# The slot stage of a decoder layer: alpha in one tile, the output product on 64 rows, the division on ScalarE, gelu ahead of the exponential

## The chip, the core and the metric

The kernel runs on one core of a Trainium2 chip. The metric is the device time of one execution in microseconds. The times are medians of repeated executions; a profile is one further execution, with its own time.

## What is computed

A decoder layer on 64 sequences of 128 tokens with 256 features: `x` plus local and latent attention, plus cross attention, plus a slot layer. The change touches the slot layer only, whose input is the normalised `x`:

```python
S = slot_init * slot_scale                      # 64 slots x 256
h = gelu(concat(x, mean(S)) @ w1.T + b1)        # 128 hidden
route_logits = (h @ w2.T + b2) / (abs(tau) + 0.1)
topk_vals, topk_idx = top_k(route_logits, 8)
topk_w = softmax(topk_vals)
alpha = sum(topk_w[..., None] * one_hot(topk_idx, 64), axis=-2)   # tokens x slots
slot_input = einsum('bts,btd->bsd', alpha, x)
gi = slot_input / (alpha.sum(axis=1) + 1e-08)
r, z = sigmoid(xr + hr), sigmoid(xz + hz)       # from gi @ w_ih and S @ w_hh
n = tanh(xn + r * hn)
S_new = (1 - z) * n + z * S
slot_values = S_new @ wv.T + bv
out = einsum('bts,bsd->btd', alpha, slot_values) @ wo.T + bo
```

The layer's result is `x + out`.

## The kernel before

The program has three stages that follow each other on one core: the first attention, the cross attention (its engines end their work some 1479 us after the span's start) and the slot stage, `slots` (L1830 to L2320). `x` stays in SBUF as `x_sb`, [128 tokens, 64 sequences, 256]. The activation and weight tiles are f32.

`slots` first has a block that makes constants: the initial slots, their share in the gates (`rz_const`, `half_hn`, `n_const`), the product `w_vo` of the value and output weights and the value bias through the output weights, `b_vo`. Both halves of the 128 partitions hold the 64 slots, one half for each of two sequences.

Then comes the loop. One step handles pairs of sequences: 32 pairs, and the step for pair `at` also does later parts of the work for the pairs one to four steps back (`at.back(k)`). The functions `step` on each engine set the order by hand; each engine runs its own list in program order, and semaphores join them. `pairs` (L79) unrolls the first eight steps, runs a hardware loop with four steps in its body (`BY = 4`), and unrolls the rest, with `LAST` more steps in which only the older pairs have work.

The life of a pair: VectorE takes the statistics of `x` and scales it to `xn` (L2160), TensorE transposes it (L2021), ScalarE copies it out (`f_xn_t`, L2090), TensorE makes the hidden product (L2029) and ScalarE the gelu (`h_t`, L2101). One step later TensorE makes the logits (L2012); VectorE scales them (L2181), finds the eight largest of each half (`max`, L2187), negates the largest (`neg_top`, L2192) and marks the chosen (L2194); ScalarE takes the exponential (`expd`, L2119); VectorE masks (`chosen`, L2201), sums, inverts, and writes `alpha` (L2211). Two steps back, TensorE makes the slot inputs (L2004), VectorE divides them (`gi`, L2171), TensorE transposes `alpha` (L2049) and `gi` (L2055), ScalarE copies both (`alpha_t`, L2106; `gi_t`, L2112), TensorE makes the gate products (L2063), and VectorE adds the constants (`rz`, L2217). Three steps back, ScalarE takes the tanh (`rz_t`, L2126), GpSimd makes `r_hn` and `r_hn_c` (L2294, L2297), VectorE `n_in` (L2229), ScalarE its tanh `n_out` (L2131), GpSimd `h_n` (L2302), VectorE `z_hn` and `slot_new` (L2233, L2237). Four steps back, TensorE transposes the new slots, multiplies with `w_vo` (L2042), VectorE adds `b_vo` (`slot_val`, L2176), TensorE makes the output (L2072), VectorE adds `x_bias` and writes `y` (L2223), and SyncE stores it (L1991).

`alpha` of one pair is a [128, 2, 128] tile, in which the half that belongs to the other sequence is zero; so its transpose has two blocks of 128 columns, and the output product runs over 128 rows. `x_bias` is `x` plus the output bias, made by GpSimd (L2306). The order of ScalarE's list is this:

```python
for back, what in ((3, gates), (0, copy_xn), (4, copy_slots), (2, copy_alpha),
                   (2, copy_inputs), (3, candidate), (1, exp), (0, gelu)):
```

`gates` is `rz_t` and `candidate` is `n_out`. Between functions whose tables differ the compiler puts an `ACT_TABLE_LOAD`, under the line of the activation that needs it.

Of the kernel before, what the change touches and what calls it, by code (L numbers as in the profile page):

```python
# [7 lines left out]
ALU = mybir.AluOpType  # L8
# [83 lines left out]
def decoder(nc, a, out):  # L92
    with ExitStack() as ctx:
# [12 lines left out]
        with ExitStack() as kept:  # L106
# [6 lines left out]
            with ExitStack() as scope:  # L113
                slots(nc, scope, sem, a, out, bank, x_sb, ident, slot_weights)
# [1715 lines left out]
def slots(nc, scope, sem, a, out, bank, x_sb, ident, w):  # L1830
# [20 lines left out]
    b_vo = sb("b_vo", [128, D])  # L1851
# [38 lines left out]
    x_bias = sb("f_x_bias", [128, 2, D])  # L1890
# [4 lines left out]
    with nc.Block() as block:  # L1895
        @block.vector
        def _(dve):
# [3 lines left out]
            nc.vector.memset(alpha_all[:], 0.0).then_inc(prep_v, 1)  # L1901
# [5 lines left out]
            nc.vector.scalar_tensor_tensor(tau_abs[:], w.tau[:], -1.0, w.tau[:], ALU.mult, ALU.max).then_inc(prep_v, 1)  # L1907
            dve.wait_ge(prep_v, 6)
            nc.vector.tensor_scalar(tau_abs[:], tau_abs[:], 0.1, None, ALU.add).then_inc(prep_v, 1)
            dve.wait_ge(prep_v, 7)  # L1910
            nc.vector.reciprocal(inv_tau[:], tau_abs[:]).then_inc(prep_v, 1)
            dve.wait_ge(prep_v, 8)
# [17 lines left out]
            nc.vector.tensor_copy(b_vo[:], bank[6][:, 0:D]).then_inc(prep_v, 1)  # L1930
            dve.wait_ge(prep_v, 19)

        @block.tensor
        def _(pe):
            pe.wait_ge(prep_v, 4)
# [7 lines left out]
            pe.wait_ge(prep_v, 11)  # L1943
# [15 lines left out]
    tr_bank, hid_bank, logit_bank, in_bank, gate_bank, new_bank, out_bank = (  # L1959
        bank[0], bank[1], bank[2], bank[3], bank[4:6], bank[6], bank[7])  # L1960
# [18 lines left out]
    LAST = 4  # L1979
# [3 lines left out]
    with nc.Block() as block:  # L1983

        @block.sync
        def _(sp):
            def step(at):
                give = at.back(4)
# [9 lines left out]
        def _(pe):  # L1998
            def slot_inputs(at):
                pe.wait_ge(alpha_ready, at.count(2, 2))  # L2000
                wait(pe, giT_ready, at.count(1, 0))
                for tt in range(2):
                    half = slice(SLOTS * tt, SLOTS * tt + SLOTS)
                    mm = pe.matmul(in_bank[half, 0:XW], alpha[at.par][:, tt, half], xn[at.off % BY][:, tt, :],  # L2004
# [81 lines left out]
        def _(act):  # L2086
# [16 lines left out]
            def copy_alpha(at):  # L2103
                act.wait_ge(alphaT_filled, at.count(1, 1))
                wait(act, out_filled, at.count(1, 1 - BY))
                nc.scalar.activation(alpha_t[at.off % BY][:].rearrange("p t n -> p (t n)"), out_bank[:, 0:256],  # L2106
                                     ACT.Copy).then_inc(alphaT_ready, 1)

# [33 lines left out]
        def _(dve):  # L2142
# [21 lines left out]
            def mean_inputs(at):  # L2164
                dve.wait_ge(in_filled, at.count(1, 1))
                nc.vector.tensor_scalar(w_sum[:], in_bank[:, D:XW], 1e-8, None, ALU.add).then_inc(in_step, 1)
                dve.wait_ge(in_step, at.count(3, 1))
                nc.vector.reciprocal(w_inv[:], w_sum[:]).then_inc(in_step, 1)
                dve.wait_ge(in_step, at.count(3, 2))
# [222 lines left out]
```

## Time and profile before

| what | value |
|---|---|
| median of 3 runs | 1788.61 us (1787.81 to 1790.47) |
| the profiled execution's own time | 1789.42 us |
| its span, first to last instruction | 1787.0 us |
| mean granted TensorE clock | 0.972 |
| busy: PE, DVE, ACT, POOL | 1612.1, 1367.5, 967.2, 946.1 us |

The profile names the engines PE (TensorE, with PEld for its weight loads), DVE (VectorE), ACT (ScalarE), POOL (GpSimd) and SP (SyncE). Busy times are sums over the whole span; a stage has to be read from its own stretch. In a timeline a row gives the start, the duration, the engine and line, the operation and its tiles, and in brackets how long the engine had been idle before and what released it. `x4` behind a row says that four records were merged. An f32 matmul has two records.

### The profile page before, as it was taken

What the parts mean: (1) busy time and instruction counts of PE and PEld (TensorE: products, weight loads), DVE (VectorE), ACT (ScalarE), POOL (GpSimd) and SP (SyncE); (2) the same over time, 40 slices, a digit from 0 to 9 for tenths busy, and PEclk for the clock granted to TensorE, in tenths of its full rate; (3) what the DMA queues carried; (4) which work ended last, traced back from release to release, by engine and by line L of the source; (5) the groups of instructions that cost most, each with busy time, mean ns of one, the idle gap of its engine ahead of it and who ended that gap; (6) DMA issues with size and microseconds to landing.
All of it is one profiled execution on the core that took longest, in us unless ns stands there. A gap on an engine that the chain in (4) does not pass through costs nothing. (4 is left out here: it accounts for less than half of the span.)

```text
span 1787.0 us, 52814 instructions
## 1 busy us (share of the span) xinstructions
PE 1612.1 (90%) x18272; PEld 1162.9 (65%) x18334; DVE 1367.5 (77%) x3280; ACT 967.2 (54%) x2049; POOL 946.1 (53%) x1205
## 2 busy tenths in 40 slices
PE   2799999999999999999699999999999976999997
PEld 1566666666666666666477777777777754666664
DVE  4688898989898989898356666666666644898996
ACT  1355555554555555555256565656565633777774
POOL 2345454545555555554336666666666662445544
PEclk9899999999999999999799999999999976999998
DMA  5554455545554455444210000000000000001001
GB/s 102 81 85 87 84 84 84 88 82 83 84 90 82 80 85 91 82 73 80 72 45 14 18 12 18 12 18 12 18 12 18 7 2 1 25 30 35 29 29 41
DMA packets 124323, 92.64 MB, mean 52 GB/s; under 512 B 34849, under 2 KB 122850, under 8 KB 124258
## 3 DMA queue, kind: packets, MB, share of 16 engines
q1 hardware_dynamic: 124258, 91.80, 28.1%
q8 instruction: 38, 0.62, 0.2%
q14 instruction: 27, 0.22, 0.1%
HBM read 23.06 MB, written 8.39 MB: 18 GB/s over the span
## 5 line engine op out<-in xcount | busy, mean ns | idle before, releaser
L1205 POOL TENSOR_SCALAR_AFFINE_SELECT probs_t<-probs_t 128x512 f32<-128x512 f32 x256 | 186.5, 743 | 220.7 <-ACT probs_t L894 220.6
L1682 DVE TENSOR_REDUCE c_neg_max<-score_banks 128x16 f32<-128x2048 f32 x64 | 146.5, 2290 | 100.4 <-PE score_banks L1459 100.3
L1610 ACT ACTIVATE c_probs_t<-score_banks 128x512 f32<-128x512 f32 x256 | 132.2, 603 | 66.0 <-PE score_banks L1485 66.0
L1791 POOL TENSOR_SCALAR_AFFINE_SELECT c_probs_t<-c_probs_t 128x512 f32<-128x512 f32 x256 | 155.4, 643 | 11.8 <-ACT c_probs_t L1610 11.7
L564 PE MATMUL score_banks<-xn_t,w_qk_a 128*128 128x256 f32 x512 | 133.7, 395 | 0.7 <-ACT xn_t L803 0.7
L1482 PE MATMUL score_banks<-c_q_f,c_k_z 32*128 32x128 f32 x2048 | 106.4, 307 | 22.0 <-ACT c_max_t L1603 15.4
L1482 PEld LDWEIGHTS score_banks<-c_q_f,c_k_z 32*128 32x128 f32 x2048 | 92.1, 188 | 45.3 <-ACT c_probs_t L1610 20.1
L713 PE MATMUL bank<-probs_t,v_heads 128*32 128x128 f32 x2048 | 109.2, 285 | 2.7 <-POOL probs_t L1205 0.8
L1042 DVE TENSOR_REDUCE neg_max<-score_banks 128x4 f32<-128x512 f32 x128 | 87.6, 684 | 21.3 <-PE score_banks L625 21.2
L894 ACT ACTIVATE probs_t<-bank 128x512 f32<-128x512 f32 x128 | 76.1, 595 | 41.4 <-PE bank L700 41.3
L564 PEld LDWEIGHTS score_banks<-xn_t,w_qk_a 128*128 128x128 f32 x512 | 91.6, 194 | 10.0 <-ACT xn_t L803 1.1
L1802 POOL TENSOR_TENSOR c_scaled<-c_normed,gamma 128x512 f32<-128x512 f32 x32 | 40.7, 1271 | 97.2 <-DVE c_normed L1665 97.2
L894 ACT ACTIVATE probs_t<-score_banks 128x512 f32<-128x512 f32 x128 | 76.1, 594 | 26.1 <-PE score_banks L700 25.9
L1042 DVE TENSOR_REDUCE neg_max<-bank 128x4 f32<-128x512 f32 x128 | 87.7, 685 | 2.6 <-PE bank L625 1.0
L1696 DVE TENSOR_TENSOR c_v_raw<-bank,b_v_b 128x512 f32<-128x512 f32 x32 | 22.1, 691 | 87.8 <-PE bank L1421 77.9
L2294 POOL TENSOR_TENSOR r_hn<-rz_t,half_hn 128x256 f32<-128x256 f32 x32 | 23.4, 731 | 124.0 <-ACT rz_t L2126 124.0
L2063 PE MATMUL bank<-w_ih,gi_t 128*128 128x512 f32 (+1 forms) x256 | 88.4, 488 | 0.4 <-DVE n_in L2229 0.2
L599 PE MATMUL score_banks<-w_v_a,xn_t 128*128 128x336 f32 x256 | 87.4, 464 | 0.3 <-ACT lat_raw L848 0.3
L1616 ACT ACTIVATE c_av_t<-bank 128x512 f32<-128x512 f32 x64 | 40.0, 625 | 77.7 <-PE bank L1499 77.7
L1572 ACT ACTIVATE c_k_z<-bank,b_k_half,row_half 128x256 f32<-128x256 f32 x128 | 61.9, 564 | 33.1 <-PE bank L1403 33.1
L1016 DVE TENSOR_TENSOR qk_rest<-qk_f,qk_part 128x512 f32<-128x512 f32 x64 | 74.9, 1170 | 6.1 <-ACT qk_f L829 6.1
L1499 PE MATMUL bank<-c_probs_t,c_v_heads 128*32 128x128 f32 x2048 | 74.4, 281 | 2.5 <-POOL c_probs_t L1791 1.8
(266 smaller groups left out, 4692.9 us busy)
## 6 DMA issues: line engine op xcount, KB each, us to landing
q_stack<-qk_part SPq DMA_DIRECT2D x192, 128.0 KB, 3.5
k_stack<-qk_part SPq DMA_DIRECT2D x192, 128.0 KB, 4.6
c_ctx_in<-in_ctx SPq DMA_DIRECT2D x32, 256.0 KB, 2.7
out<-y SPq DMA_DIRECT2D x32, 256.0 KB, 2.1
x_sb<-in_x SPq DMA_DIRECT2D x30, 256.0 KB, 2.7
rq_stack<-lat_part SPq DMA_DIRECT2D x192, 32.0 KB, 2.3
rk_stack<-lat_part SPq DMA_DIRECT2D x192, 16.0 KB, 1.9
w_ih<-in_ffn_w_ih SPq DMA_DIRECT2D x1, 768.0 KB, 5.8
```

The costliest lines, as they stand in the source:

```text
L564: mm = pe.matmul(dst, w(c), src[:, c, :], start=(c == 0), stop=(c == C - 1))
L599: mm = pe.matmul(v_bank[tt][:, 0:n], src[:, c, S * tt:S * tt + S], w_v[:, c, :], start=(c == 0), stop=(c == C - 1))
L713: mm = pe.matmul(av_bank[HW * j:HW * j + HW, 128 * (g % 4):128 * (g % 4) + 128], v_heads[at.par][:, tt, h0 + j, :], probs_t[g % 4][:, j, : ...
L894: nc.scalar.activation(probs_t[g % 4][:].rearrange("p j t -> p (j t)"), score_bank[g % 2][:], ACT.Exp, scale=SCALE).then_inc(exp_done, 1)
L1016: nc.vector.tensor_tensor(rest, src, part[0], ALU.subtract).then_inc(part_step, 1)
L1042: nc.vector.tensor_reduce(neg_max[:, tt, h0:h0 + 4], score_bank[g % 2][:].rearrange("p (j k) -> p j k", k=128), AX.X, ALU.max, negate=True ...
L1205: nc.gpsimd.affine_select(out=pt[:], in_=pt[:], pattern=[[0, 4], [1, 128]], compare_op=ALU.is_ge, fill=0.0, base=-1 if local else 0, chann ...
L1482: pe.matmul(slot(i, j), k_z[at.par][j // 2][group(i), j % 2, toks], q_f[at.par][group(i), j % 2, toks], start=True, stop=False, skip_group ...
L1610: nc.scalar.activation(probs_t[tt][:, 4 * g:4 * g + 4, :].rearrange("p j q -> p (j q)"), score_banks[:, g, :], ACT.Exp, scale=SCALE).then_ ...
L1682: nc.vector.tensor_reduce(neg_max[:, tt, :], all_scores, AX.X, ALU.max, negate=True).then_inc(max_done, 1)
L1791: nc.gpsimd.affine_select(out=heads, in_=heads, pattern=[[0, 4], [1, 128]], compare_op=ALU.is_ge, fill=0.0, base=0, channel_multiplier=-1) ...
L2063: mm = pe.matmul(gate_bank[b][:, 0:hi - lo], gi_t[:, c, :], w.w_ih[:, c, lo:hi], start=(c == 0), stop=(c == C - 1))
```

## The change

In the change the other half of `alpha` is no longer kept: `alpha` is [128, 2, 64], its two halves side by side are one [128, 128] tile, and one transpose gives both, the first sequence's slots on rows 0 to 63 and the second's on rows 64 to 127. The transpose goes into the bank of the slot inputs, behind those of `gi`. The output product of each sequence uses its 64 rows and a bank of its own (`out_bank` is banks 2 and 3; the logits share a bank with the hidden product). The output bias is added to the slot values (`b_all`), and `y` adds `x_sb` itself; GpSimd's `bias_x` goes, and GpSimd negates the largest logit. The division by `w_sum` moves from VectorE to ScalarE (`scale_inputs`). All lists are in a new order, and the output is made five steps back.

```diff
-    b_vo = sb("b_vo", [128, D])
+    b_all = sb("b_all", [128, D])
...
-    alpha_all = sb("alpha", [128, 2, 2, PS])
-    alpha = [alpha_all[:, i, :, :] for i in range(2)]
-    alpha_t = [sb(f"alpha_t{i}", [128, 2, 128]) for i in range(4)]
+    alpha = [sb(f"alpha{i}", [128, 2, SLOTS]) for i in range(2)]
+    alpha_t = [sb(f"alpha_t{i}", [128, 128]) for i in range(4)]
...
-            nc.vector.memset(alpha_all[:], 0.0).then_inc(prep_v, 1)
...
-            nc.vector.tensor_copy(b_vo[:], bank[6][:, 0:D]).then_inc(prep_v, 1)
+            nc.vector.tensor_tensor(b_all[:], bank[6][:, 0:D], w.b_o[:], ALU.add).then_inc(prep_v, 1)
...
-            def transpose_alpha(at):
-                wait(pe, y_ready, at.count(1, -2))
-                for tt in range(2):
-                    mm = pe.transpose(out_bank[:, 128 * tt:128 * tt + 128], alpha[at.par][:, tt, :], ident[:])
-                mm.then_inc(alphaT_filled, 1)
             def transpose_inputs(at):
-                pe.wait_ge(in_step, at.count(3, 3))
+                pe.wait_ge(gi_ready, at.count(1, 1))
                 for c in range(C):
-                    mm = pe.transpose(in_bank[:, PS * c:PS * c + PS], gi[:, 128 * c:128 * c + 128], ident[:])
-                mm.then_inc(giT_filled, 1)
+                    pe.transpose(in_bank[:, PS * c:PS * c + PS], gi[:, 128 * c:128 * c + 128], ident[:])
+                pe.transpose(in_bank[:, 2 * PS:3 * PS], alpha[at.par][:].rearrange("p t n -> p (t n)"),
+                             ident[:]).then_inc(giT_filled, 1)
...
             def give_out(at):
                 pe.wait_ge(val_ready, at.count(1, 1))
-                later = 3 if at.back(-2).real else 2 if at.back(-1).real else 1
-                pe.wait_ge(alphaT_ready, at.count(1, later))
-                for tt in range(2):
-                    mm = pe.matmul(out_bank[:, D * tt:D * tt + D], alpha_t[at.off % BY][:, tt, :], slot_val[:],
+                pe.wait_ge(alphaT_ready, at.count(1, 1))
+                wait(pe, y_ready, at.count(1, 0))
+                for tt in range(2):
+                    half = slice(SLOTS * tt, SLOTS * tt + SLOTS)
+                    mm = pe.matmul(out_bank[tt][:, 0:D], alpha_t[at.off % BY][half, :], slot_val[half, :],
                                    start=True, stop=True, skip_group_check=True)
...
-                for back, what in ((2, slot_inputs), (1, route), (0, transpose_x), (4, transpose_slots),
-                                   (2, transpose_alpha), (2, transpose_inputs), (0, hidden), (4, slot_values),
-                                   (2, gates), (4, give_out)):
+                for back, what in ((1, route), (0, transpose_x), (5, give_out), (2, slot_inputs), (4, transpose_slots),
+                                   (0, hidden), (2, transpose_inputs), (4, slot_values), (2, gates)):
...
+            def scale_inputs(at):
+                act.wait_ge(in_step, at.count(2, 2))
+                wait(act, giT_filled, at.count(1, 0))
+                nc.scalar.activation(gi[:], in_bank[:, 0:D], ACT.Copy, scale=w_inv[:, 0:1]).then_inc(gi_ready, 1)
...
-                for back, what in ((3, gates), (0, copy_xn), (4, copy_slots), (2, copy_alpha),
-                                   (2, copy_inputs), (3, candidate), (1, exp), (0, gelu)):
+                for back, what in ((3, gates), (0, copy_xn), (4, copy_slots), (2, scale_inputs), (3, candidate),
+                                   (2, copy_inputs), (2, copy_alpha), (0, gelu), (1, exp)):
...
-                nc.vector.tensor_scalar(gi[:], in_bank[:, 0:D], w_inv[:, 0:1], None, ALU.mult).then_inc(in_step, 1)
...
-                nc.vector.tensor_scalar(neg_top[:], top[:, :, 0], -1.0, None, ALU.mult).then_inc(negtop_ready, 1)
+                dve.sem_inc(dve_turn, 1)
...
-                nc.vector.tensor_tensor(y[at.par][:], out_bank[:].rearrange("p (t d) -> p t d", t=2), x_bias[:],
-                                        ALU.add).then_inc(y_ready, 1)
+                nc.vector.tensor_tensor(y[at.par][:], score_banks[:, 2:4, 0:D],
+                                        x_sb[:, bass.ds(at.row, 2), :], ALU.add).then_inc(y_ready, 1)
...
-            def bias_x(at):
-                wait(pool, y_ready, at.count(1, 0))
-                nc.gpsimd.tensor_tensor(x_bias[:], x_sb[:, bass.ds(at.row, 2), :],
-                                        w.b_o[:].unsqueeze(1).to_broadcast([128, 2, D]), ALU.add).then_inc(xb_ready, 1)
+            def negate_top(at):
+                pool.wait_ge(top_ready, at.count(1, 1))
+                wait(pool, exp_ready, at.count(1, 0))
+                pool.sem_inc(pool_turn, 1)
+                nc.gpsimd.tensor_scalar(neg_top[:], top[:, :, 0], -1.0, None, ALU.mult).then_inc(negtop_ready, 1)
```

GpSimd calls `negate_top` between `reset_gate` and `one_over_deviation`.

ScalarE, one step in the hardware loop's body, before (`h_t` is the gelu, `expd` the exponential, `n_out` the candidate's tanh):

```order
L2126 ACTIVATE rz_t<-rz 128x512
L2088 REGISTER_ALU
L2090 ACTIVATE f_xn_t<-score_banks 128x512
L2095 ACTIVATE slot_new_t<-bank 128x256
L2106 ACTIVATE alpha_t<-bank 128x256
L2112 ACTIVATE gi_t<-score_banks 128x256
L2131 ACTIVATE n_out<-n_in 128x256
L76 REGISTER_ALU
L2119 ACT_TABLE_LOAD
L2119 ACTIVATE expd<-logits,neg_top 128x64 x2
L2101 ACT_TABLE_LOAD
L2101 ACTIVATE h_t<-score_banks,b_all 128x256
```

The same step of the change:

```order
L2129 ACTIVATE rz_t<-rz 128x512
L2086 REGISTER_ALU
L2088 ACTIVATE f_xn_t<-score_banks 128x512
L2093 ACTIVATE slot_new_t<-bank 128x256
L2108 REGISTER_ALU
L2110 ACTIVATE gi<-bank,w_inv 128x256
L2134 ACTIVATE n_out<-n_in 128x256
L2115 ACTIVATE gi_t<-bank 128x256
L2104 ACTIVATE alpha_t<-bank 128x128
L2099 ACT_TABLE_LOAD
L2099 ACTIVATE h_t<-score_banks,b_all 128x256
L2122 ACT_TABLE_LOAD
```

Behind the last row stand the two `expd`, then the next step's `rz_t`. There are two table loads in each order; in the second the gelu and its load stand between `n_out` and the exponential, and the two copies stand behind `n_out`. In the change the load under L2099 carries the wait for an earlier product of logits, the load under L2122 that for an earlier `alpha`.

VectorE from `rz` to `n_in` before:

```order
L2217 TENSOR_TENSOR rz<-bank,rz_const 128x512
L2223 TENSOR_TENSOR y<-bank,f_x_bias 128x512
L2166 TENSOR_SCALAR w_sum<-score_banks 128x1
L2168 RECIPROCAL w_inv<-w_sum 128x1
L2171 TENSOR_SCALAR gi<-score_banks,w_inv 128x256
L2181 SCALAR_TENSOR_TENSOR logits<-score_banks,inv_tau,b 128x128
L2153 BN_AGGR f_moments<-f_stats 128x2 x2
L2229 TENSOR_TENSOR n_in<-bank,r_hn_c 128x256
```

And in the change:

```order
L2218 TENSOR_TENSOR rz<-bank,rz_const 128x512
L2182 SCALAR_TENSOR_TENSOR logits<-score_banks,inv_tau,b 128x128
L2156 BN_AGGR f_moments<-f_stats 128x2 x2
L2188 MAX top<-logits 128x8 x2
L2169 TENSOR_SCALAR w_sum<-bank 128x1
L2172 RECIPROCAL w_inv<-w_sum 128x1
L2195 MATCH_REPLACE rest<-top,logits 128x64 x2
L2223 TENSOR_TENSOR y<-score_banks,x_sb 128x512
L2229 TENSOR_TENSOR n_in<-bank,r_hn_c 128x256
```

`max` and the marking have come ahead of `n_in`, and `gi` has left. In both orders `rz` stands right behind the two `alpha` instructions; behind `n_in` the change has the statistics, `f_xn`, `z_hn`, `slot_new`, `slot_val`, `chosen`, its sum and inverse, and `alpha`.

## Rows read from the trace of the kernel before

**Rows 1.** Windows of core 0: length; busy PE, PEld, DVE, ACT, POOL; PE clock, DMA.

```profile
1540.00:1640.00 100.00, 93.12 (x452) 64.64 (x452) 90.12 (x348) 72.87 (x132) 51.40 (x72) 1.00 0.09 32
...
1515.00:1523.00 8.00, 6.20 (x32) 3.60 (x28) 6.73 (x28) 5.82 (x10) 3.04 (x5) 1.00 0.00 1
...
1772.00:1780.00 8.00, 4.75 (x14) 2.80 (x14) 3.79 (x6) 1.55 (x4) 4.67 (x5) 0.70 0.18 63
```

**Rows 2.** Tile `rz`: durations in ns, first and last start in us.

```profile
L2217 DVE TENSOR_TENSOR rz<-bank,rz_const x32: 681/683/692, 1514.7 to 1771.1; 128x512 f32<-128x512 f32 x32
```

**Rows 3.** Chain that ended last: start us, us, what.

```profile
1532.18 0.75 POOL r_hn L2294
...
1733.70 0.74 POOL r_hn L2294
```

**Rows 4.** DVE waits from 1540 to 1740: total us, times, longest.

```profile
DVE n_in L2229 <- POOL r_hn_c L2297: 13.3, 24, 0.7
```

**Rows 5.** Timeline, one step of the loop: start us, us, engine, line, operation.

```profile
1606.40 0.68 DVE L2217 TENSOR_TENSOR rz<-bank,rz_const 128x512 f32<-128x512 f32 x1
...
1607.12 0.63 ACT L2126 ACTIVATE rz_t<-rz 128x512 f32<-128x512 f32 x1 [0.61 <-DVE rz L2217]
...
1607.83 0.73 POOL L2294 TENSOR_TENSOR r_hn<-rz_t,half_hn 128x256 f32<-128x256 f32 x1 [3.85 <-ACT rz_t L2126]
...
1607.98 0.48 DVE L2171 TENSOR_SCALAR gi<-score_banks,w_inv 128x256 f32<-128x256 f32 x1
...
1608.64 0.73 POOL L2297 TENSOR_TENSOR r_hn_c<-r_hn,n_const 128x256 f32<-128x256 f32 x1
...
1609.02 0.39 ACT L2106 ACTIVATE alpha_t<-bank 128x256 f32<-128x256 f32 x1
1609.29 0.40 ACT L2112 ACTIVATE gi_t<-score_banks 128x256 f32<-128x256 f32 x1
...
1609.40 0.42 DVE L2229 TENSOR_TENSOR n_in<-bank,r_hn_c 128x256 f32<-128x256 f32 x1 [0.52 <-POOL r_hn_c L2297]
...
1609.86 0.42 ACT L2131 ACTIVATE n_out<-n_in 128x256 f32<-128x256 f32 x1 [0.17 <-DVE n_in L2229]
...
1610.40 0.33 DVE L2187 MAX8 top<-logits 128x8 f32<-128x64 f32 x2
...
1611.19 1.28 ACT L2119 ACT_TABLE_LOAD   x1 [0.92 <-DVE neg_top L2192]
...
1611.40 0.41 DVE L2176 TENSOR_TENSOR slot_val<-bank,b_vo 128x256 f32<-128x256 f32 x1
...
1612.49 0.59 ACT L2119 ACTIVATE expd<-logits,neg_top 128x64 f32<-128x64 f32 x2
...
1613.10 1.28 ACT L2101 ACT_TABLE_LOAD   x1
...
1613.32 1.03 PE L2072 MATMUL bank<-slot_val,alpha_t 128*128 128x256 f32 x4
1613.51 0.35 DVE L2201 SCALAR_TENSOR_TENSOR chosen<-rest,expd 128x64 f32<-128x64 f32 x2
...
1614.39 0.47 ACT L2101 ACTIVATE h_t<-score_banks,b_all 128x256 f32<-128x256 f32 x1
1614.41 0.42 DVE L2211 TENSOR_SCALAR alpha<-chosen,chosen_inv 128x64 f32<-128x64 f32 x2
1614.75 0.68 DVE L2217 TENSOR_TENSOR rz<-bank,rz_const 128x512 f32<-128x512 f32 x1
```

**Rows 6.** Timeline of ACT and DVE, second step of the stage.

```profile
1503.92 0.59 ACT L2119 ACTIVATE expd<-logits,neg_top 128x64 f32<-128x64 f32 x2
...
1504.62 0.36 DVE L2201 SCALAR_TENSOR_TENSOR chosen<-rest,expd 128x64 f32<-128x64 f32 x2 [0.50 <-ACT expd L2119]
```

**Rows 7.** Timeline of ACT, fourth step of the stage.

```profile
1518.21 0.42 ACT L2131 ACTIVATE n_out<-n_in 128x256 f32<-128x256 f32 x1 [0.70 <-DVE n_in L2229]
1518.64 1.28 ACT L2119 ACT_TABLE_LOAD   x1
```

More of the change, by code:

```diff
@@ L113, in decoder @@
             with ExitStack() as scope:
-                slots(nc, scope, sem, a, out, bank, x_sb, ident, slot_weights)
+                slots(nc, scope, sem, a, out, score_banks, bank, x_sb, ident, slot_weights)
 class SlotWeights:
@@ L1827, in _, with slots @@
             pairs(pool, step, TAIL, ahead=1)
-def slots(nc, scope, sem, a, out, bank, x_sb, ident, w):
+def slots(nc, scope, sem, a, out, score_banks, bank, x_sb, ident, w):
     def sb(name, shape, dt=F32):
@@ L1889, in slots @@
     slot_val = sb("slot_val", [128, D])
-    x_bias = sb("f_x_bias", [128, 2, D])
     y = [sb(f"y{i}", [128, 2, D]) for i in range(2)]
@@ L1978, in slots @@
     BY = 4
-    LAST = 4
+    LAST = 5
     with nc.Block() as block:
@@ L1987, in step @@
             def step(at):
-                give = at.back(4)
+                give = at.back(5)
                 if give.real:
@@ L2001, in slot_inputs @@
                 wait(pe, giT_ready, at.count(1, 0))
+                wait(pe, alphaT_ready, at.count(1, 0))
                 for tt in range(2):
                     half = slice(SLOTS * tt, SLOTS * tt + SLOTS)
-                    mm = pe.matmul(in_bank[half, 0:XW], alpha[at.par][:, tt, half], xn[at.off % BY][:, tt, :],
+                    mm = pe.matmul(in_bank[half, 0:XW], alpha[at.par][:, tt, :], xn[at.off % BY][:, tt, :],
                                    start=True, stop=True, skip_group_check=True)
@@ L2027, in hidden @@
                 wait(pe, hid_ready, at.count(1, 0))
+                wait(pe, logit_ready, at.count(1, 0))
                 for c in range(C):
@@ L2103, in copy_alpha @@
             def copy_alpha(at):
-                act.wait_ge(alphaT_filled, at.count(1, 1))
+                act.wait_ge(giT_filled, at.count(1, 1))
                 wait(act, out_filled, at.count(1, 1 - BY))
-                nc.scalar.activation(alpha_t[at.off % BY][:].rearrange("p t n -> p (t n)"), out_bank[:, 0:256],
+                nc.scalar.activation(alpha_t[at.off % BY][:], in_bank[:, 2 * PS:3 * PS],
                                      ACT.Copy).then_inc(alphaT_ready, 1)
+            def scale_inputs(at):
+                act.wait_ge(in_step, at.count(2, 2))
+                wait(act, giT_filled, at.count(1, 0))
+                nc.scalar.activation(gi[:], in_bank[:, 0:D], ACT.Copy, scale=w_inv[:, 0:1]).then_inc(gi_ready, 1)
             def copy_inputs(at):
@@ L2166, in mean_inputs @@
                 nc.vector.tensor_scalar(w_sum[:], in_bank[:, D:XW], 1e-8, None, ALU.add).then_inc(in_step, 1)
[L2167 removed]
+                dve.wait_ge(in_step, at.count(2, 1))
+                wait(dve, gi_ready, at.count(1, 0))
                 nc.vector.reciprocal(w_inv[:], w_sum[:]).then_inc(in_step, 1)
[L2169 to L2171 removed]
             def slot_values(at):
@@ L2175, in slot_values @@
                 wait(dve, out_filled, at.count(1, 0))
-                nc.vector.tensor_tensor(slot_val[:], new_bank[:, 0:D], b_vo[:], ALU.add).then_inc(val_ready, 1)
+                nc.vector.tensor_tensor(slot_val[:], new_bank[:, 0:D], b_all[:], ALU.add).then_inc(val_ready, 1)
             def route_logits(at):
@@ L2208, in route_weights @@
                 dve.wait_ge(pick_step, at.count(4, 4))
-                wait(dve, alphaT_filled, at.count(1, -1))
+                wait(dve, giT_filled, at.count(1, -1))
                 for tt in range(2):
-                    nc.vector.tensor_scalar(alpha[at.par][:, tt, SLOTS * tt:SLOTS * tt + SLOTS], chosen[:, tt, :],
+                    nc.vector.tensor_scalar(alpha[at.par][:, tt, :], chosen[:, tt, :],
                                             chosen_inv[:, tt:tt + 1], None, ALU.mult).then_inc(alpha_ready, 1)
@@ L2242, in step @@
                 norms = at.real and following.real
-                routed, fed, updated, given = (at.back(k) for k in (1, 2, 3, 4))
+                routed, fed, updated, renewed, given = (at.back(k) for k in (1, 2, 3, 4, 5))
                 if norms:
@@ L2246, in step @@
                     dve.wait_ge(xn_ready, at.count(1, 1))
-                if fed.real:
-                    mean_inputs(fed)
+                if updated.real:
+                    gates(updated)
                 if routed.real:
@@ L2252, in step @@
                     norm_moments()
+                if routed.real:
+                    dve.wait_ge(logit_ready, routed.count(1, 1))
+                    dve.sem_inc(dve_turn, 1)
+                    route_top(routed)
+                if fed.real:
+                    mean_inputs(fed)
+                if routed.real:
+                    route_mark(routed)
+                if given.real:
+                    output(given)
                 if updated.real:
                     candidate(updated)
-                if routed.real:
-                    dve.wait_ge(logit_ready, routed.count(1, 1))
                 if at.real and second.real:
@@ L2268, in step @@
                     new_slots(updated)
+                if renewed.real:
+                    slot_values(renewed)
                 if routed.real:
                     route_weights(routed)
-                if fed.real:
-                    gates(fed)
-                if given.real:
-                    output(given)
             norm_stats(At(0, 0))
```

40 lines of the change are left out of this document (18 added, 22 removed).

## The prediction

> **What bounds the kernel now.** I read the windows first, to see which stage the change touches, then the first and last addition `rz`, then the waits of VectorE, and last the timeline of one step. The change is in the slot stage alone, the last 290 us of a span of 1787.0 us. There [rows 1] show a loop that fills no engine: in 100 us TensorE is busy 93.12, VectorE 90.12, ScalarE 72.87, GpSimd 51.40, at a granted clock of 1.00. So the question is what closes the circle from one step to the next. `rz` is written 32 times, from 1514.7 to 1771.1 [rows 2]: 31 turns in 256.4 us. Inside the loop `r_hn` starts at 1532.18 and 24 steps later at 1733.70 [rows 3], so a turn is 201.52 / 24 = 8.40 us. In one turn [rows 5] the starts are: `rz` 1606.40, ScalarE's tanh `rz_t` 1607.12 (+0.72), GpSimd's `r_hn` 1607.83 (+0.71), `r_hn_c` 1608.64 (+0.81), VectorE's `n_in` 1609.40 (+0.76), and then VectorE's own queue without a pause up to the next `rz` at 1614.75 (+5.35): 8.35 in all. The only steady wait of VectorE is the one before `n_in`, 24 times, 13.3 us in 200 [rows 4], 0.52 in the step shown. The bound is a ring through four engines, most of it VectorE's queue: 8.35 - 0.52 = 7.83 us of VectorE's instructions a step.
>
> In this ring ScalarE's `exp` ends at 1613.08 and `chosen` starts at 1613.51 [rows 5]: the exponential is ready 0.43 us early. `gelu`, with its table load (1613.10, 1.28 us), comes after it and delays nobody. This is the cover that the change takes away.
>
> **Part by part.** *VectorE.* It loses `gi` (0.48 long, and `gi_t`'s chain moves to ScalarE; at most 0.40 of queue) and `neg_top` (about 0.24 of the 1.00 between `max` at 1610.40 and `slot_val` at 1611.40). What is left is 7.83 - 0.40 - 0.24 = 7.2 us. That would be the gain, if VectorE's queue set the turn.
>
> *From `rz` to `n_in`.* The ring's first four edges stay: 0.72 + 0.71 + 0.81 + 0.76 = 3.00. Does VectorE arrive in time? Today it has 3.00 - 0.52 = 2.48 of work there. The new order takes `gi` out (-0.40) and puts `max` and the marking in (at most 1.00 - 0.24 = 0.76): 2.84. It waits some 0.15, and GpSimd still ends last.
>
> *`y` and the biases.* `f_x_bias` leaves GpSimd, whose new `neg_top` comes right behind `r_hn_c`, so it is done well before the ScalarE queue wants it. `y` reads `x_sb` in place of `x_bias` at the same size. I cost both at nothing; the cover is the wait of VectorE found below. Putting `b_o` into `b_all` is one addition in place of one copy, before the loop: nothing.
>
> *TensorE.* Output products on 64 rows in two banks: today four records in 1.03 us [rows 5]; the bounds are nothing and half of it, -0.5. One transpose less of `alpha`: some -0.1. TensorE works 93.12 / 100 x 8.40 = 7.8 us a step, so even with no gain it has room in the step below. Nothing on the path. What it is moved past: `give_out` now stands ahead of `slot_inputs` and asks for the previous step's `slot_val`, long written.
>
> *ScalarE: the step that counts.* The order is now `rz_t`, `f_xn_t`, `slot_new_t`, `gi` (the new division), `n_out`, `gi_t`, `alpha_t`, table load, `gelu`, table load, `exp`. Tables are loaded twice a step, as before; but both loads and `gelu` now lie between `n_out` and `exp`. The queue is served in order, and `n_out` cannot start before `n_in`. The starts from there on:
> - `n_in` to `n_out` 0.46 (1609.40, 1609.86) [rows 5];
> - `n_out` to `gi_t` 0.30: a copy starts 0.12 before the one ahead ends (`alpha_t`, 0.39 long, and `gi_t` 0.27 later), and `n_out` lasts 0.42;
> - `gi_t` to `alpha_t` 0.40 - 0.12 = 0.28;
> - `alpha_t` to the load 0.28: a copy of 128 columns instead of 256. 512 columns take 0.63 and 256 take 0.39, so I take 0.27; bounds 0.15 and 0.39. A load does not overlap: it starts 0.01 after the end of what is ahead [rows 7];
> - load to `gelu` 1.29, `gelu` to the second load 0.47 + 0.01, load to `exp` 1.30 [rows 5];
> - `exp` to `chosen` 0.70, where VectorE is waiting for it [rows 6]; if that row is untypical, 0.59 + 0.05;
> - `chosen` to `alpha` 0.90, `alpha` to the next `rz` 0.34 [rows 5]: in VectorE's new order `rz` is the first of a step and stands right behind `alpha`.
>
> The new ring: 3.00 + 0.46 + 0.30 + 0.28 + 0.28 + 1.29 + 0.48 + 1.30 + 0.70 + 0.90 + 0.34 = **9.33 us**. A turn in the loop is 0.05 above the step read today (8.40 to 8.35), for the loop's own instructions; I keep that: 9.38. VectorE needs 4.11 from `n_in` to `chosen` today, 1.00 less without `max` and marking, so 3.11; ScalarE's way is 5.09. VectorE will stand about 2.0 us a step before `chosen`, and 9.33 - 7.2 agrees.
>
> *The division on ScalarE.* Between `slot_new_t` and `n_out`, where ScalarE waits for `n_in` anyway. A 256-column activation with an operand by row takes 0.47 (`gelu`, rows 5); from `rz` on, `rz_t` begins at 0.72 and three more follow, so it ends near 2.5, ahead of 3.46. Its late effect is on TensorE's `gates`: they start near 4.2, end near 6.9 and are wanted at 9.3. Nothing.
>
> **The sum.** 29 turns hold a full ring (the turns with a `gelu` in them): 29 x 9.38 = 272.0. The last two have no table load and no `gelu`: between 9.33 - 3.07 = 6.3 and today's 7.8; I take 7.0, since `h_n` and `slot_new` bound them: 14.0. Together 286.0 against 256.4: +29.6. The first `rz` comes later, as each `exp` of the first steps waits for the next `gelu`: 0 to +3, taken 1.0. After the last `rz` the half-size output product takes part of its 1 us away: 0 to -1.5, taken -0.5. The larger zeroing of `alpha` ahead of the stage goes: 0 to -0.5, taken -0.4. Sum +29.7 on the profiled execution's 1789.42 us: 1819.1. The median of the runs is 0.8 lower, 1788.61; so **1818**.
>
> **The rivals.**
> *Faster: the loads hide.* Behind the change each load carries an old wait only, the late ones stand on the activation. If ScalarE ran its loads under waits, or needed one less, VectorE's queue would decide. One load less: 9.38 - 1.29 = 8.09, 29 x 8.09 + 14.0 - 256.4 = -7.8, 1781 us. Both gone: 7.2, -33.6, 1755. The turning point for no loss is a chain 1.0 us shorter than I read it, for the full gain 2.1. Against it: `n_out` stands ahead of both loads in an in-order queue, and [rows 7] show a load behind `n_out`, not beside it. 5 in 100.
> *No change.* Several edges shorter together by 1.0: nothing in the rows says so. 3 in 100.
> *The clock falls.* TensorE is busy about 7.3 of 9.38, 0.78. At 0.59 busy the clock was 0.70; but at 6.20 of 8.00, also 0.78, it was 1.00 [rows 1]. If a quarter of the steps ran at 1.2 GHz, 14.6 us of matmuls each, that is 7 x 5.2 = +37, 1855. 5 in 100.
> *A switch costs more than its load.* In [rows 5] the activation behind a load starts 1.29 to 1.30 after it, and the load takes 1.28: no more is paid. With 1.38 more for each, the ring would be 12.09 and the time 29 x 2.76 = 80 longer, 1898. 2 in 100. That figure is the Trainium skill's, page "ScalarE: Activation LUTs", section "What ACT_TABLE_LOAD costs": about 1283 ns for the load and 1380 ns of drain, 2.66 us a switch. By that rule the sum would be 1898 and not 1818; the trace agrees with the load's length and shows no drain behind it.
>
> **How the numbers follow.** The forecast has 85 in 100. Its own range: shorter edges (`exp` to `chosen` 0.06, `alpha_t` 0.12, the loop's 0.05) give -6.7, short last turns and an early first `rz` another -2.4: 1809. Upward, VectorE reaching `n_in` 0.25 late gives +7, the start and the last turns +3.6: 1829, and 1830 with a little of the clock. A measurement tells 0.2%, some 3.6 us, from no change. Slower 0.92 (85 + 5 + 2), same 0.03, faster 0.05.
>
> **What would show it.** Right: `chosen` waits for `expd` some 2 us a step, over 50 us in all; two loads with one `gelu` between them and `exp` behind; `r_hn` every 9.3 to 9.4 us; VectorE near 76% busy in the loop; the wait for `neg_top` on ScalarE gone. Wrong: turns under 8.4, a load that starts before `n_out` ends, another wait on VectorE longer than that for `exp`, or a clock under 0.95 in the loop.

## The result and the profile after

The changed kernel takes 1828.47 us (median of 4 runs, 1826.7 to 1829.9), the kernel before 1788.75 us; the ratio is 1.022, with a 95% interval from 1.0203 to 1.0238. It is slower, as forecast. It lies 10 us above the forecast of 1818 and 1.5 us below the upper end of the range. The profiled execution took 1826.70 us with a span of 1825.0 and a mean clock of 0.967.

The windows of the changed kernel's loop, with the columns of [rows 1]:

```profile
1540.00:1640.00 100.00, 84.38 (x388) 54.38 (x389) 73.47 (x275) 66.24 (x125) 32.46 (x61) 0.95 0.08 28
1640.00:1740.00 100.00, 82.03 (x380) 52.40 (x378) 74.27 (x284) 63.56 (x122) 32.22 (x61) 0.95 0.08 26
```

TensorE and VectorE are busy less than before, 84.38 and 73.47 of 100 us against 93.12 and 90.12, GpSimd 32.46 against 51.40 since `x_bias` is gone. Less work, and more time: something in the ring waits. New is the clock, 0.95 in place of 1.00. The tile `rz`, as in [rows 2], and the longest waits from 1540 to 1740 us, in the form of [rows 4]:

```profile
L2218 DVE TENSOR_TENSOR rz<-bank,rz_const x32: 682/683/692, 1516.0 to 1810.0; 128x512 f32<-128x512 f32 x32
```

```profile
ACT rz_t L2129 <- DVE rz L2218: 45.7, 21, 2.6
DVE chosen L2202 <- ACT expd L2122: 39.8, 21, 2.6
...
ACT n_out L2134 <- DVE n_in L2229: 20.0, 20, 1.1
...
DVE n_in L2229 <- POOL r_hn_c L2298: 5.6, 20, 0.4
...
ACT gi_t L2115 <- PE bank L2053: 3.3, 6, 0.8
```

`rz` now takes 294.0 us from its first to its last start, 256.4 before. VectorE's wait for the exponential ahead of `chosen`, which did not stand among its waits before, is 39.8 us in 21 turns, 1.9 a turn. ScalarE idles 2.07 us ahead of `rz_t`, and its wait for `neg_top` is no longer there. Now one turn in the timeline, to be held against [rows 5]; between `chosen` and `alpha` the sum and its inverse are left out:

```profile
1622.60 0.68 DVE L2218 TENSOR_TENSOR rz<-bank,rz_const 128x512 f32<-128x512 f32 x1
...
1623.32 0.63 ACT L2129 ACTIVATE rz_t<-rz 128x512 f32<-128x512 f32 x1 [2.07 <-DVE rz L2218]
...
1624.02 0.73 POOL L2295 TENSOR_TENSOR r_hn<-rz_t,half_hn 128x256 f32<-128x256 f32 x1 [6.41 <-ACT rz_t L2129]
...
1624.48 1.13 PE L2033 MATMUL score_banks<-f_xn_t,w 128*128 128x256 f32 x4 [0.72 <-ACT f_xn_t L2088]
...
1624.83 0.73 POOL L2298 TENSOR_TENSOR r_hn_c<-r_hn,n_const 128x256 f32<-128x256 f32 x1
...
1625.59 0.42 DVE L2229 TENSOR_TENSOR n_in<-bank,r_hn_c 128x256 f32<-128x256 f32 x1 [0.25 <-POOL r_hn_c L2298]
...
1626.05 0.42 ACT L2134 ACTIVATE n_out<-n_in 128x256 f32<-128x256 f32 x1 [0.98 <-DVE n_in L2229]
1626.38 0.37 ACT L2115 ACTIVATE gi_t<-bank 128x256 f32<-128x256 f32 x1
1626.64 0.27 ACT L2104 ACTIVATE alpha_t<-bank 128x128 f32<-128x128 f32 x1
...
1626.93 1.28 ACT L2099 ACT_TABLE_LOAD   x1
...
1628.22 0.47 ACT L2099 ACTIVATE h_t<-score_banks,b_all 128x256 f32<-128x256 f32 x1
...
1628.71 1.28 ACT L2122 ACT_TABLE_LOAD   x1
...
1630.01 0.59 ACT L2122 ACTIVATE expd<-logits,neg_top 128x64 f32<-128x64 f32 x2
...
1630.70 0.36 DVE L2202 SCALAR_TENSOR_TENSOR chosen<-rest,expd 128x64 f32<-128x64 f32 x2 [1.71 <-ACT expd L2122]
...
1631.61 0.42 DVE L2212 TENSOR_SCALAR alpha<-chosen,chosen_inv 128x64 f32<-128x64 f32 x2
1631.94 0.68 DVE L2218 TENSOR_TENSOR rz<-bank,rz_const 128x512 f32<-128x512 f32 x1
```

From `rz` to `rz` it is 9.34 us, and the start of each row is set by the one above it (TensorE's hidden product, at 1624.48, stands beside the chain). Between `n_out` and the exponential lie 3.96 us of ScalarE's own queue, with both loads and the gelu in it; in [rows 5] this way was 2.63, of which 0.92 was a wait for `neg_top`.

### The profile page after: what moved, and what is told of

It reads as the page before. It is cut to its first block and busy times, and to the rows that moved or that the text cites. A ratio compares the mean times of both kernels' runs of the same rounds, so it can differ in the third digit from the quotient of the medians.

```text
span 1825.0 us, 52814 instructions
## 1 busy us (share of the span) xinstructions
PE 1613.7 (88%) x18240; PEld 1151.7 (63%) x18302; DVE 1349.9 (74%) x3215; ACT 970.3 (53%) x2079; POOL 911.3 (50%) x1205
## 5 line engine op out<-in xcount | busy, mean ns | idle before, releaser
L1042 DVE TENSOR_REDUCE neg_max<-score_banks 128x4 f32<-128x512 f32 x128 | 87.6, 684 | 19.9 <-PE score_banks L625 19.7
L2061 PE MATMUL bank<-w_ih,gi_t 128*128 128x512 f32 (+1 forms) x256 | 92.4, 504 | 2.5 <-ACT gi_t L2115 2.2
L2061 PEld LDWEIGHTS bank<-w_ih,gi_t 128*128 128x128 f32 x256 | 48.1, 195 | 45.9 <-issue 31.7
```

The lines of the kernel that those rows point to most:

```text
L1042: nc.vector.tensor_reduce(neg_max[:, tt, h0:h0 + 4], score_bank[g % 2][:].rearrange("p (j k) -> p j k", k=128), AX.X, ALU.max, negate=True ...
L2061: mm = pe.matmul(gate_bank[b][:, 0:hi - lo], gi_t[:, c, :], w.w_ih[:, c, lo:hi], start=(c == 0), stop=(c == C - 1))
```

## The experiments

All turns below are distances between starts of `rz_t` in the timeline; "mean" is the mean of the first 29. The kernel before has 8.345 (7.67 the first, 7.81 the last, 8.33 to 8.51 between), the changed one 9.651. A ratio is to the kernel before as measured beside the run in question, whose median lay between 1786.95 and 1789.14 us. Two theories stood against each other at the start. A: the ring through `n_out`, the two copies, load, gelu, load and exponential sets the turn. B: the gelu's place is harmless, and the loss comes from the clock and the moved work of TensorE.

| kernel | median us | ratio to before, 95% interval | mean turn us |
|---|---|---|---|
| changed | 1828.47 | 1.022 (1.0203 to 1.0238) | 9.651 |
| e1, exponential first again | 1796.95 | 1.006 (1.0043 to 1.0077) | 8.688 |
| e2, before with the gelu first | 1808.69 | 1.0126 (1.0109 to 1.0143) | 8.960 |
| e3, no table loads | 1764.73 | 0.9873 (0.9857 to 0.989) | 7.633 |
| e4, TensorE filled | 1824.32 | 1.0215 (1.0198 to 1.0233) | 9.452 |
| e10, filled, long loop body | 1822.18 | 1.0197 (1.0183 to 1.0211) | 9.353 |
| e5, gelu ahead of `n_out` | 1783.61 | 0.9971 (0.9961 to 0.9981) | 8.230 |
| e9, ScalarE's list | 1797.81 | 1.0047 (1.003 to 1.0064) | 8.675 |
| e7, ScalarE's and TensorE's lists | 1765.35 | 0.9872 (0.9856 to 0.9889) | 7.688 |
| e8, four lists | 1763.62 | 0.9868 (0.9851 to 0.9885) | 7.678 |
| e11, e8 with a long loop body | 1762.69 | 0.9867 (0.9851 to 0.9882) | 7.640 |

### Is it the gelu's place and the table loads?

**e1** undoes the one exchange in the changed kernel:

```diff
-                                   (2, copy_inputs), (2, copy_alpha), (0, gelu), (1, exp)):
+                                   (2, copy_inputs), (2, copy_alpha), (1, exp), (0, gelu)):
```

> The changed kernel with one thing undone: on ScalarE the exponential stands ahead of the gelu again, all else as in the change. Theory A (the ring through n_out, gi_t, alpha_t, table load, gelu, table load, exp, chosen, alpha, rz sets the turn): gelu and its load leave the way to exp, the ring read from the rows falls below other chains, and the next one is gelu to route, logits, max, n_in, n_out and back, some 8.55 us a turn: about 1.1 less than the 9.65 the changed kernel shows, so 1796, at most 1805 if the clock still falls. Theory B (the position of the gelu is harmless; the loss comes from the longer clock falls and the moved work of TensorE): turns stay at 9.3 or more, 1820 to 1828.

1796.95 us, theory A's 1796. This alone gives back 31.5 of the change's 39.7 us; 10.0 us over the kernel before, as measured beside it, are left. The clock in the loop is 1.00 again. `chosen` no longer waits; VectorE's longest waits are now on TensorE, behind the gelu:

```profile
DVE w_sum L2169 <- PE bank L2007: 18.2, 23, 0.8
DVE logits L2182 <- PE score_banks L2015: 10.2, 23, 0.5
```

The mean turn is 8.69, 0.14 over the 8.55 expected.

**e2** makes the same exchange in the kernel before, and nothing else:

```diff
-                                   (2, copy_inputs), (3, candidate), (1, exp), (0, gelu)):
+                                   (2, copy_inputs), (3, candidate), (0, gelu), (1, exp)):
```

> The kernel before with one part of the change alone: gelu ahead of the exponential on ScalarE. Theory A: the ring n_in, n_out 0.46, load 0.43, gelu 1.29, load 0.48, exp 1.30, chosen 0.70, alpha 0.90, rz 0.34, and 3.00 back to n_in: 8.9 us a turn against 8.40, so 1789 + 29 x 0.5 = 1803; chosen waits for expd about 0.5 us a step. Theory B: no change, 1789.

1808.69 us, where A said 1803 and B 1789: 19.9 us over the 1788.75 of the result, 21.7 over the kernel before as measured beside it. The steady turn is 8.91, the 8.9 expected, and `chosen` waits 0.5 us. Against the kernel before this is 8.91 - 8.34 = 0.57 a turn, 16.5 us in 29 turns, where the expectation counted 0.5; on the mean of the turns it is 0.615, 17.8 us. The chain in the timeline of ScalarE, and VectorE's wait:

```profile
1600.67 0.42 ACT L2131 ACTIVATE n_out<-n_in 128x256 f32<-128x256 f32 x1 [0.25 <-DVE n_in L2229]
1601.10 1.28 ACT L2101 ACT_TABLE_LOAD   x1
1602.39 0.48 ACT L2101 ACTIVATE h_t<-score_banks,b_all 128x256 f32<-128x256 f32 x1
1602.89 1.28 ACT L2119 ACT_TABLE_LOAD   x1
1604.18 0.59 ACT L2119 ACTIVATE expd<-logits,neg_top 128x64 f32<-128x64 f32 x2
```

```profile
DVE chosen L2201 <- ACT expd L2119: 10.8, 23, 0.5
```

Moving the gelu costs some 20 us in the old arrangement too. It costs 31.5 in the new one, where `gi_t` and `alpha_t` (0.33 + 0.26) also stand behind `n_out`, and where the clock falls besides (below); how the difference divides was not isolated.

**e3** takes the loads away by taking the gelu's function away:

```diff
-                nc.scalar.activation(h_t[:], hid_bank[:, 0:PT], ACT.Gelu, bias=b1_all[:, 0:1]).then_inc(hid_ready, 1)
+                nc.scalar.activation(h_t[:], hid_bank[:, 0:PT], ACT.Tanh, bias=b1_all[:, 0:1]).then_inc(hid_ready, 1)
```

> The changed kernel with the hidden layer's gelu replaced by a tanh, which shares its table with the exponential: the loop has no table load; what is left out is the gelu function itself, so the output is another. Theory A: 2.58 us leave the ring, 9.34 becomes 6.8, and another chain takes over at 7.2 to 7.5 us (VectorE's queue): 29 turns are 2.15 shorter, 1828 - 62 = 1766. Theory B (the loads are hidden): 1828.

1764.73 us; A said 1766. In ScalarE's queue:

```profile
1601.74 0.42 ACT L2134 ACTIVATE n_out<-n_in 128x256 f32<-128x256 f32 x1 [0.75 <-DVE n_in L2229]
...
1602.84 0.59 ACT L2122 ACTIVATE expd<-logits,neg_top 128x64 f32<-128x64 f32 x2
```

From `n_out` to the exponential it is 1.10 us, against 3.96: 2.86 less, the two loads (2 x 1.28) and 0.30 by which the activations now overlap. The loads were on the path with their full length. The turn fell by less, to a steady 7.54, where the next bound is. This bound is not ScalarE:

```profile
1540.00:1640.00 100.00, 98.61 (x487) 62.41 (x486) 93.42 (x353) 46.09 (x130) 42.02 (x81) 1.00 0.10 35
```

TensorE 98.61 and VectorE 93.42 of 100 us: with the ring out of the way the change's savings show for the first time. B has fallen.

### Where do the turns above 9.34 come from?

Of the changed kernel's first 29 turns 12 are 9.33 to 9.36, the others 9.42 to 10.68. Some of its windows, cut at starts of `rz_t`, with the columns of [rows 1]:

```profile
1516.72:1526.05 9.33, 5.79 (x29) 3.65 (x27) 6.25 (x26) 5.97 (x11) 3.20 (x6) 1.00 0.00 1
1526.05:1536.28 10.23, 9.51 (x35) 6.54 (x33) 6.64 (x27) 6.35 (x12) 3.20 (x6) 0.67 0.00 0
1536.28:1545.62 9.34, 8.36 (x45) 4.92 (x41) 7.20 (x28) 6.35 (x12) 3.22 (x6) 1.00 0.09 30
1545.62:1555.74 10.12, 9.08 (x39) 6.13 (x37) 7.14 (x28) 6.35 (x12) 3.21 (x6) 0.83 0.08 27
...
1593.44:1604.12 10.68, 9.43 (x41) 6.36 (x39) 7.32 (x28) 6.35 (x12) 3.21 (x6) 0.84 0.08 26
1604.12:1613.54 9.42, 7.30 (x36) 4.60 (x35) 6.99 (x28) 6.24 (x12) 3.21 (x6) 1.00 0.08 28
```

Eight of the 17 long turns, 9.72 to 10.68, have a low clock, 0.67 once and 0.82 to 0.84 otherwise. The other nine, 9.42 to 9.86, run at 1.00 and need another cause, which e4 and e10 show. Inside the turn that starts at 1545.62, TensorE's hidden product and transpose of `alpha`, and the copies that wait:

```profile
1546.79 1.97 PE L2033 MATMUL score_banks<-f_xn_t,w 128*128 128x256 f32 x4 [0.72 <-ACT f_xn_t L2088]
...
1548.36 0.42 ACT L2134 ACTIVATE n_out<-n_in 128x256 f32<-128x256 f32 x1 [0.98 <-DVE n_in L2229]
...
1548.98 0.42 PE L2053 MATMUL bank<-ident,alpha 128*128 128x128 f32 x1
...
1549.44 0.39 ACT L2115 ACTIVATE gi_t<-bank 128x256 f32<-128x256 f32 x1 [0.67 <-PE bank L2053]
```

The hidden product took 1.97 us, against 1.13 in the fast turn above, where it starts at 1624.48. So the transposes come late, and `gi_t` starts 1.08 us behind `n_out` and not 0.33. The ring runs through TensorE in such a turn: `f_xn_t`, hidden product, transposes, `gi_t`, and on as before.

**e4** keeps TensorE busy with matmuls that nobody reads, ahead of the output product and of the hidden product:

```diff
+                for _ in range(2):
+                    pe.matmul(out_bank[1][:, 256:512], w.w_ih[:, 0, 0:128], w.w_ih[:, 0, 0:256],
+                              start=True, stop=True, skip_group_check=True)
...
+                for _ in range(2):
+                    pe.matmul(hid_bank[:, 384:512], w.w_ih[:, 0, 0:128], w.w_ih[:, 0, 0:128],
+                              start=True, stop=True, skip_group_check=True)
```

> The changed kernel with four more matmuls a step that nobody reads, in the two places where TensorE stands idle: two of 256 columns ahead of the output product, two of 128 ahead of the hidden product. Theory C (the turns of 9.4 to 10.7 us, a third of all, come from steps at the lower clock, in which transposes and copies reach n_out and gi_t late): the clock stays at 1.00, every turn is 9.34, and the time falls by 29 x 0.31 = 9 us to 1819. Theory D (they come from the loop's own instructions or from the order): the time stays at 1828 or rises with the added work, with the clock at 1.00.

```profile
1540.00:1640.00 100.00, 96.23 (x480) 63.15 (x479) 75.83 (x290) 64.54 (x126) 33.77 (x64) 1.00 0.08 27
```

The clock is 1.00, TensorE does 12 us more work in 100, and in the profiled execution (1819.31 us) no turn is over 9.88. That is theory C for the eight turns with a low clock. The median, 1824.32, fell by 4 us and not by 9, and its interval overlaps the changed kernel's: the other three runs took 1822.6 to 1826.1, with a mean clock of 0.973 to 0.978 against 0.979. Whether falls were left in their loops isn't shown: e10 below has 1.00 in every turn of its profile at a mean of 0.975. The changed kernel's four runs had 0.963 to 0.967. One turn in four is still 9.82 to 9.88, with 9.42 behind it, as in theory D. At such a turn VectorE's timeline shows this (the pass ends between the first two rows):

```profile
1597.85 0.42 DVE L2218 TENSOR_SCALAR alpha<-chosen,chosen_inv 128x64 f32<-128x64 f32 x2
1598.64 0.69 DVE L2224 TENSOR_TENSOR rz<-bank,rz_const 128x512 f32<-128x512 f32 x1 [0.38 <-issue]
...
1607.82 0.42 DVE L2218 TENSOR_SCALAR alpha<-chosen,chosen_inv 128x64 f32<-128x64 f32 x2
1608.15 0.68 DVE L2224 TENSOR_TENSOR rz<-bank,rz_const 128x512 f32<-128x512 f32 x1
```

`alpha` to `rz` is 0.79 in place of 0.33, with 0.38 put down to "issue".

**e10** is e4 with a body of eight steps in the slot stage's hardware loop:

```diff
-            pairs(pe, step, LAST, by=BY)
+            pairs(pe, step, LAST, by=8)
```

and the same on the other four engines.

> The kernel with four more matmuls a step that nobody reads, and the hardware loop's body of the slot stage eight steps long in place of four. With four, every fourth turn of that kernel was 9.82 to 9.88 and the one behind it 9.42, against 9.34: 0.6 us a pass. If that is the loop's end (VectorE's branch and register instructions now stand between alpha and rz, on the ring): with one or two passes in place of five or six, at most two or three turns are long and the time falls by some 4 x 0.6 = 2.4 us, to 1820 to 1822. If it is something that recurs every four steps (four buffers): unchanged, 1824, with the long turns still at every fourth.

The long turns at every fourth step are gone: 26 of 29 are 9.33 to 9.35, the longest 9.49. The five runs lie between 1821.77 and 1822.31. VectorE's loop runs once there, in place of five times, so it never jumps back. So it was the loop's end, some 0.6 us a pass; what in it takes the time was not isolated. The tile `rz`:

```profile
L2224 DVE TENSOR_TENSOR rz<-bank,rz_const x32: 681/684/693, 1516.4 to 1802.0; 128x512 f32<-128x512 f32 x32
```

1802.0 - 1516.4 = 285.6 us for the 31 turns. The medians of e4 and e10 are 2.1 us apart, as expected, but with overlapping intervals; the turns tell them apart, not the medians.

### Does the ring tell where the gelu should stand?

If A holds, the same addition of rows through all four queues should tell the time of other orders. Four were tried, all from the changed kernel.

**e5**:

```diff
-                for back, what in ((3, gates), (0, copy_xn), (4, copy_slots), (2, scale_inputs), (3, candidate),
-                                   (2, copy_inputs), (2, copy_alpha), (0, gelu), (1, exp)):
+                for back, what in ((3, gates), (0, copy_xn), (4, copy_slots), (2, scale_inputs), (0, gelu),
+                                   (2, copy_inputs), (3, candidate), (1, exp), (2, copy_alpha)):
```

> The changed kernel with ScalarE's list in another order: the gelu right behind the division, ahead of n_out; alpha_t behind the exponential. One load and the gelu leave the stretch between n_out and exp; they run while ScalarE waits for n_in. Theory A (the ring from n_in to chosen): the chain becomes f_xn_t, hidden product, gelu, gi_t, n_out, load, exp, about 8.1 us a turn plus 0.15 for the loop, 8.2: 29 x 1.4 = 41 less than 1828, 1787, and up to 1795 if clock falls remain. If instead every table load costs its place wherever it stands: about 9.3 a turn, 1820.

1783.61 us: faster than the kernel before, by 0.3%.

```profile
1608.32 0.42 ACT L2134 ACTIVATE n_out<-n_in 128x256 f32<-128x256 f32 x1
1608.75 1.28 ACT L2122 ACT_TABLE_LOAD   x1
1610.05 0.59 ACT L2122 ACTIVATE expd<-logits,neg_top 128x64 f32<-128x64 f32 x2
```

The gelu still comes ahead of the exponential here, but from `n_out` to the exponential it is 1.73 us in place of 3.96; the two copies have left this stretch too. What costs is not that order but the length of the stretch behind `n_out`.

**e9** moves only ScalarE's list, **e7** TensorE's too:

```diff
-                for back, what in ((3, gates), (0, copy_xn), (4, copy_slots), (2, scale_inputs), (3, candidate),
-                                   (2, copy_inputs), (2, copy_alpha), (0, gelu), (1, exp)):
+                for back, what in ((0, copy_xn), (3, gates), (4, copy_slots), (2, scale_inputs), (2, copy_inputs),
+                                   (2, copy_alpha), (3, candidate), (1, exp), (0, gelu)):
...
-                for back, what in ((1, route), (0, transpose_x), (5, give_out), (2, slot_inputs), (4, transpose_slots),
+                for back, what in ((0, transpose_x), (5, give_out), (1, route), (2, slot_inputs), (4, transpose_slots),
```

> The changed kernel with ScalarE's list as f_xn_t, rz_t, slot_new_t, division, gi_t, alpha_t, n_out, exp, gelu; nothing else moved. Theory A: exp now comes 0.45 + one load behind n_out, the first ring falls to about 7.5, but the ring through gelu, logits, TensorE's gates (which stand ahead of the logits' product in TensorE's queue) and gi_t takes over at 8.4 a turn, 8.55 with the loop: 1795. Rival: with ScalarE relieved, VectorE's 7.2 to 7.6 sets the turn: 1765.

> As the run with ScalarE's list alone, and TensorE's list with the transposes of x and the output product ahead of the logits' product. Theory A with the chains added from rows: 7.5 us a turn, 7.65 with the loop, 29 x 7.65 + 14 = 236 against 256.4 before: 1767. If TensorE's order does not matter: the same as that run.

e9 gives 1797.81: the ring through `n_out` is gone, and ScalarE waits for TensorE instead, as its waits show:

```profile
ACT f_xn_t L2088 <- PE score_banks L2024: 28.3, 23, 1.3
ACT gi_t L2115 <- PE bank L2053: 14.6, 23, 0.6
```

`f_xn_t` waits 28.3 us for the transposes of `x`, which stand behind the logits' product, which waits for the gelu. With the transposes ahead of it (e7) the time is 1765.35, 2 us from the 1767 expected. This order beats both kernels, by 1.3% the one before and by 3.5% the changed one. Its windows and its tile `rz`:

```profile
1540.00:1640.00 100.00, 97.97 (x481) 62.80 (x481) 92.90 (x351) 82.33 (x156) 41.98 (x78) 1.00 0.10 35
1640.00:1740.00 100.00, 96.72 (x473) 61.06 (x471) 89.02 (x339) 80.30 (x153) 40.15 (x74) 1.00 0.10 34
```

```profile
L2218 DVE TENSOR_TENSOR rz<-bank,rz_const x32: 681/683/692, 1508.4 to 1745.5; 128x512 f32<-128x512 f32 x32
```

TensorE and VectorE are busy more than 96 and 89 of 100 us at a clock of 1.00: the change's savings have become time.

**e8** adds two small moves, `norm_moments` ahead of `route_logits` on VectorE and the addition of epsilon ahead of `reset_gate` on GpSimd, and **e11** gives it the loop's body of eight steps.

> As the run with two lists, and two small moves: VectorE aggregates the statistics ahead of the logits, GpSimd adds epsilon ahead of r_hn. By the chains 7.4 against 7.5 us a turn: 1764, 3 us less; no difference if VectorE's queue is full at 7.5.

> The kernel with the lists of four engines reordered, with the loop's body eight steps long: one turn in four was 8.07 in place of 7.6 there. If that is the loop's end, four of them go: 1763.6 - 4 x 0.45 = 1762; if not, 1763.6.

1763.62 and 1762.69 us. Both go the way expected, by 1.7 and 0.9 us, and neither is told from e7 by its interval.

## Why the prediction was right, and where 10 us were missing

**What held.** Each edge of the new ring was within 0.03 us of its row: `n_out` to `gi_t` 0.33 (0.30 said), `gi_t` to `alpha_t` 0.26 (0.28), to the load 0.29 (0.28), load to gelu 1.29 (1.29), gelu to the second load 0.49 (0.48), load to the exponential 1.30 (1.30), to `chosen` 0.69 (0.70), to `alpha` 0.91 (0.90), to `rz` 0.33 (0.34); the sum 9.34 against 9.33. The copy of 128 columns, priced by a slope at 0.27, took 0.27. `n_in` waited 0.25 for GpSimd (0.15 said), so VectorE's queue did not end last there. `chosen` waited 1.9 us (2.0 said), 39.8 in 21 turns. The last two turns took 14.17 (14.0 said). Of the signs named beforehand, the turn of 9.3 to 9.4 us came in 12 turns of 29, VectorE was busy 73.5 and 74.3 in 100 (76 said), and the clock in the loop, 0.95, stood right at the bound under which it was to speak against the forecast. The output product went from 1.03 to 0.70 us and the division took 0.48 on ScalarE; neither shows in the turn, as said. e1, e2 and e3 show the cause from three sides: take the gelu out of the stretch, put it into the old kernel's, or take the loads out.

**What was mis-sized.** Measured on the profiled executions, the first `rz_t` came 1.25 us later (1.0 - 0.4 = 0.6 said), the 31 turns took 37.7 us more (29.6 said), the end 0.9 less (0.5 said), and the time outside the span fell by 0.7. That the start came near is luck: the stage's own constants (`rz_const`) began 1.9 us earlier than in the kernel before, at 1487.51 against 1489.43, and e2, which is the kernel before up to there, has 1487.85; from them to the first `rz_t` it took 3.2 us more, where 1.0 was said and at most 3. The term that fell short is the 9.38 a turn, 9.33 and 0.05 for the loop: the mean of the 29 turns was 9.651, 7.9 us over the 272.0.
- *The loop's 0.05.* I carried it over from the kernel before. There the pass ends with `y` between `rz` and `w_sum`, work that has 0.5 us of slack ahead of `n_in`; in the change VectorE's pass ends between `alpha` and `rz`, on the ring. From e10 to e4 the mean rises by 0.10: 2.9 us in 29 turns, where 1.5 was counted.
- *The clock.* I gave its fall 5 in 100, since a stretch with 0.78 busy had run at 1.00 [rows 1]. It did fall, in part of the turns: 0.95 on the mean. From e4 to the changed kernel the mean turn rises from 9.452 to 9.651, 5.8 us in the profiled executions (4 between the medians). The rival was right that the clock falls, and about in how many turns (8 of 29, a quarter said); its price, 37 us (7 x 5.2 is 36.4), was far too high. By its clock alone a turn with a fall is 0.4 to 0.9 us longer and not 5.2 (10.68 holds the loop's end as well): the fall covers only part of the turn, whose mean clock is 0.82 to 0.84, once 0.67; TensorE has 2 us of slack behind `gates`, and only the hidden product and the transposes reach the ring.

Without both, in e10, the 29 turns take 271.2 us, 0.8 under the 272.0 of the forecast; the ring itself was priced rightly, and the 7.9 us too few are these two.

**The rivals.** A hidden load: no; in e3 the stretch from `n_out` to the exponential is shorter by both. A switch dearer than its load (1898 us, an estimate from the 1380 ns of drain that the Trainium skill gives, page "ScalarE: Activation LUTs", section "What ACT_TABLE_LOAD costs"): no; behind the first load the gelu starts 1.29 us after it, behind the second the exponential 1.30, and each load takes 1.28. Of the drain that the page adds these rows show nothing: the load starts 0.02 after the end of the activation ahead.

## What to carry to other kernels

Where the engines of a loop are each below full, follow the chain from one turn to itself and add start-to-start distances, not busy times; an instruction taken from a full queue gains nothing if the same edit lengthens the ring elsewhere. A table load costs its 1.28 us where it stands in the queue, so keep what can go elsewhere out of the stretch between the late operand and the result that the next engine waits for. In e5 and e7, the orders that beat the kernel before, one load still stands behind `n_out`; the second load and the gelu do not. After a ring is cut, look at once for the next one, and try the orders of two queues together: one list moved alone gave 1798 us, two gave 1765.

## What the runs showed of the hardware that I had not expected

- The end of a hardware loop's pass cost up to 0.46 us in VectorE's queue (`alpha` to `rz` 0.79 against 0.33) and some 0.6 us in the turn and the one behind it, where the ring runs through it, against 0.25 a pass in the kernel before (turns of 8.42 and 8.50 among those of 8.34).
- TensorE's clock can fall in a loop that keeps it busy 0.8 of the time: it was 1.00 in the turn from 1516.72 to 1526.05, with 5.79 of 9.33 us busy, and 0.67 in the next. With four useless matmuls a step it was 1.00 in every turn of the profiled execution, whose 31 turns took 5.6 us less. The execution as a whole was 7.4 us faster, but 3.1 of these lie ahead of `rz_const` (1484.45 against 1487.51), where the two kernels are the same.
- Two output products on 64 rows each, into two banks, took 0.70 us together, against 1.03 on 128 rows into one; whether the rows or the banks make it was not tried.
